# The shared expert of the last batch computed after the expert tiles of a Flamingo block, from operands kept in DRAM

## The reference, cut to what matters

```python
def _L1_ffn_ref(hidden_states, router_w, gate_w, up_w, down_w, s_gate_w, s_gate_b, s_up_w, s_up_b, s_down_w, s_down_b):
    B, S, H, I, E, TOP_K, NS = (2, 512, 512, 352, 8, 2, 2)
    ...
    logits = x @ router_w.T
    probs = jax.nn.softmax(logits.astype(jnp.float32), axis=-1)
    topk_w, topk_idx = jax.lax.top_k(probs, TOP_K)
    ...
    def expert_step(acc, ws):
        gw, uw, dw, ce = ws
        out = jax.nn.silu(x @ gw) * (x @ uw) @ dw
        return (acc + ce[:, None].astype(out.dtype) * out, None)
    moe_out, _ = jax.lax.scan(expert_step, jnp.zeros_like(x), (gate_w, up_w, down_w, combine.T))
    shared = jax.nn.silu(x @ s_gate_w + s_gate_b) * (x @ s_up_w + s_up_b) @ s_down_w + s_down_b
    return (moe_out + shared).reshape(b, s, h)
...
x = x + jnp.tanh(g_ffn[1]) * _L1_ffn_ref(_layernorm(x, axis=-1), L1_ffn_router_w, ...)
```

## Time and profile before

| | us |
|---|---|
| median of 3 runs | 1328.61 |
| lowest and highest | 1327.72, 1329.63 |
| the profiled execution's own time | 1324.98 |
| its span, first to last instruction | 1323.3 |
| PE busy | 1088.6 (82%) |
| DVE busy | 751.8 (57%) |
| ACT busy | 664.9 (50%) |
| POOL busy | 460.1 (35%) |

### The profile page before, as it was taken

How to read it: one execution, slowest core, us unless ns; L and a number is a source line. 1 busy time by engine, 2 the same in 40 slices (tenths; PEclk the granted TensorE clock), 3 DMA queues, 4 the chain that set the end, 5 groups by cost and what they waited for, 6 DMA issues and landing times. The chain is left out here.

```text
span 1323.3 us, 19258 instructions
## 1 busy us (share of the span) xinstructions
PE 1088.6 (82%) x6093; PEld 520.5 (39%) x6111; DVE 751.8 (57%) x1420; ACT 664.9 (50%) x1010; POOL 460.1 (35%) x503
## 2 busy tenths in 40 slices
PE   0567788896699999999999467899997999999910
PEld 0343444453233343243232133444444566566600
DVE  6889867756786674665653466443333435443224
ACT  6888878794156665655667154212212344334400
POOL 1102443323102332322333303435006888882054
PEclk9978899998989999999999778799998999999965
DMA  9126600001102111110110122024003454442256
GB/s 336 45 96 196 257 0 1 1 1 40 37 23 68 37 40 54 40 37 22 41 31 18 45 74 66 1 96 181 1 0 114 150 162 166 150 156 93 71 170 227
DMA packets 66573, 110.62 MB, mean 84 GB/s; under 512 B 16756, under 2 KB 28660, under 8 KB 65992
## 3 DMA queue, kind: packets, MB, share of 16 engines
q1 hardware_dynamic: 56952, 77.63, 18.2%
q0 software_dynamic: 9264, 31.92, 7.6%
q10 hardware_dynamic: 288, 0.20, 0.1%
HBM read 68.44 MB, written 33.28 MB: 77 GB/s over the span
## 5 line engine op out<-in xcount | busy, mean ns | idle before, releaser
L1240 ACT ACTIVATE prob<-p_col,mask_col,any_key 128x512 f32<-128x512 f32 x256 | 185.7, 778 | 110.4 <-PE p_col L1371 108.9
L1438 DVE CUSTOM_DVE_ANT_0 ajunk<-p_row,mask_row 128x512 bf16<-128x512 f32 x256 | 166.8, 685 | 70.8 <-PE p_row L1321 70.8
L1334 PE MATMUL p_out<-prob,v 128*64 128x512 f32 x512 | 139.0, 621 | 0.1
L1321 PE MATMUL p_row<-ks,early_place 99*128 99x512 f16 x256 | 99.3, 389 | 13.4 <-DVE top L1438 11.9
L1160 POOL TENSOR_TENSOR o<-sum_a,rec 32x512 f32<-32x512 f32 x30 | 37.9, 1264 | 195.2 <-DMA rec<-inv_d 193.0
L1371 PE MATMUL p_col<-early_place,ks 101*128 101x512 f16 x256 | 95.5, 386 | 0.7 <-ACT prob L1240 0.3
L2290 DVE SCALAR_TENSOR_TENSOR shid<-s_up,ssilu 128x352 f32<-128x352 f32 x39 | 20.5, 525 | 122.1 <-PE s_up L2236 122.1
L2258 PE MATMUL s_down<-mw,shT 128*128 (+1 forms) x351 | 82.2, 379 | 1.1 <-ACT shT L2198 1.1
L2236 PE MATMUL s_gate<-mw,sxT 128*128 x468 | 78.3, 318 | 4.2 <-ACT sxT L2204 3.3
L2236 PE MATMUL s_up<-mw,sxT 128*128 x468 | 76.7, 314 | 0.0
L1851 PE MATMUL p_gate<-mw 128*128 128x512 f16 (+1 forms) x288 | 71.7, 402 | 1.2 <-ACT mw L1737 1.2
(11 more groups left out here) (305 smaller groups left out, 2151.6 us busy)
## 6 DMA issues: line engine op xcount, KB each, us to landing
x_slots<-nought SPq DMA_DIRECT2D x3, 3328.0 KB, 19.8
xin<-x_slots SPq DMA_DIRECT2D x39, 256.0 KB, 2.7
y_slots<-y SPq DMA_DIRECT2D x39, 256.0 KB, 2.1
early_place<-in_ctx SPq DMA_DIRECT2D x8, 1024.0 KB, 5.6
mstg<-in_L_ffn_gate_w POOLq DMA_DIRECT2D x7, 704.0 KB, 5.0
mstg<-in_L_ffn_up_w POOLq DMA_DIRECT2D x7, 704.0 KB, 5.3
x<-in_x SPq DMA_DIRECT2D x4, 1024.0 KB, 6.7
w<-in_L_ffn_w SPq DMA_DIRECT2D x1, 4096.0 KB, 18.3
```

Source lines behind the costliest of these rows:

```text
L1240: nc.scalar.activation(prob[s % 4][:, c, :], p_col[c][:], ACT.Exp, bias=mask_col[:, b, k:k + 1], scale=any_key[:, b:b + 1]).then_inc(t_exp, 1)
L1321: nc.tensor.matmul(p_row[g % 2][:], qs[0:ROWS_R, j, g, t * P:(t + 1) * P], ks[b % 2][0:ROWS_R, g, :], start=True, stop=True).then_inc(t_ro ...
L1334: mm = nc.tensor.matmul(p_out[pr][c * 2 * DH:(c + 1) * 2 * DH, :], v1[b % 2][:, k, g, :], prob[n % 4][:, c, :], start=(k == 0), stop=(k == ...
L1438: nc.vector.tensor_tensor_reduce(junk[:, g % 2, :], p_row[g % 2][:], mask_row[:, blk // HPG, :], 1.0, -3e38, ALU.add, ALU.max, top[blk % 2 ...
```

## The change

The last batch (g = 3, `LATE_B`) leaves the loops of the first block on PE, ACT and DVE: its `gate_up`, `hidden`, `down` and `add` for both units are gone there. Behind its last weight load SP now writes the two split shared units and the `xT` rows of batch 3 (high and low) into two DRAM tensors, and waits for all six transfers.

In the second block the gate part of unit 0 is loaded into a tile of its own (`first_gate`) at the start. `xT` of batch 3 (`late_T`) goes into the `mstg` buffers after the last split. When PE is through with the last tile, SP loads the up part of unit 0 to the place of expert 5, stores the last `y`, and loads the rest of both units. PE, ACT and DVE then do the same products for batch 3 that stood in the first block, with hidden rows at the places of experts 4 and 7. DVE's list interleaves them with the additions of the gathered rows (`combine`). `bias` and `gate_dn` live in both blocks.

```diff
@@ stage_shared, SP: behind the weight loads
+            for u in range(2):
+                kept = w[:, (SHARED + u) * 2 * WC:(SHARED + u + 1) * 2 * WC].rearrange("p (h c) -> p h c", h=2)
+                sp.wait_ge(m_wl, NQ * (u + 1))
+                sp.dma_start(shared_d[u, :, :, 0:MAIN], kept[:, :, 0:MAIN]).then_inc(m_saved, 16)
+                sp.dma_start(shared_d[u, 0:ELAST, :, MAIN:WC], kept[0:ELAST, :, MAIN:WC]).then_inc(m_saved, 16)
+            sp.wait_ge(m_xT, NT)
+            for h in range(2):
+                sp.dma_start(late_d[h], xT[:, h, :, LATE_B * S:(LATE_B + 1) * S]).then_inc(m_saved, 16)
+            sp.wait_ge(m_saved, 16 * 6)
@@ stage_shared, PE
-            for g in range(1, B):
+            for g in range(1, LATE_B):
                 gate_up(g, 0)
                 down(g - 1, 1)
...
-            down(B - 1, 1)
+            down(LATE_B - 1, 1)
@@ stage_tiles, SP
+            sp.dma_start(first_gate[:], shared_d[0, :, :, G0:U0]).then_inc(e_pre, 16)
...
+            sp.wait_ge(m_wl, NQ * (2 + EXPERTS))
+            for h in range(2):
+                sp.dma_start(late_T[h], late_d[h]).then_inc(e_pre, 16)
             body(PAIRS_OF_TILES, 0)
+            sp.wait_ge(e_down, TILES)
+            sp.dma_start(late_w[0][:, :, U0:D0], shared_d[0, :, :, U0:D0]).then_inc(e_lu, 16)
             store(PAIRS_OF_TILES, 0)
+            sp.dma_start(late_w[1][:, :, G0:D0], shared_d[1, :, :, G0:D0]).then_inc(e_lv, 16)
+            for n, done in enumerate((e_ld0, e_ld1)):
+                sp.dma_start(late_w[n][:, :, D0:MAIN], shared_d[n, :, :, D0:MAIN]).then_inc(done, 16)
+                sp.dma_start(late_w[n][0:ELAST, :, MAIN:WC], shared_d[n, 0:ELAST, :, MAIN:WC]).then_inc(done, 16)
@@ stage_tiles, PE: behind the last tile
+            def late_gate_up(n):
...
+                        if m == 0:
+                            pe.wait_ge(*came)
+                        pe.wait_ge(free, TILES + max(c - 1, 0))
...
+            def late_down(n, done):
+                pe.wait_ge(done, 32)
+                pe.wait_ge(e_hl, TILES + EB * (n + 1))
+                for t in range(TPB):
+                    pe.wait_ge(e_y, TILES + max(TPB * n + t - 1, 0))
...
+            late_gate_up(0)
+            late_gate_up(1)
+            late_down(0, e_ld0)
+            late_down(1, e_ld1)
@@ stage_tiles, DVE: behind the last tile
+            for c in range(2 * EB):
+                late_hidden(c)
+                if c:
+                    late_low(c - 1)
+                if c == EB:
+                    combine(0)
+            late_low(2 * EB - 1)
+            combine(1)
+            late_add(0)
+            combine(2)
+            late_add(1)
+            dve.wait_ge(e_y, TILES + 2 * TPB)
+            combine(LATE_B)
```

More of the change, by code:

```diff
@@ L1791, in _ @@
             hidden(2, 1)
-            hidden(3, 0)
-            hidden(3, 1)
             act.wait_ge(m_scat, SCATTERED)
@@ L2019, in _ @@
             add(1, 0)
-            for g in range(2, B):
+            for g in range(2, LATE_B):
                 hidden(g, 0)
@@ L2031, in _, with stage_tiles @@
                     low_part(u, q)
[L2034 removed]
+def stage_tiles(nc, sb, ps, sem, st, a, x, x_slots, y_slots, out_d, w, stg, dest, share, expert_of, m_wh, m_wl,
+                bias, gate_dn, shared_d, late_d):
     NQ = len(W_PARTS)
@@ L2046, in stage_tiles @@
     identh = sb(st, "sidenth", [P, P], F16)
+    first_gate = sb(st, "first_gate", [P, 2, KB * EI], F16)
+    late_T = [stg[h][:, 0:KB * S // 2].bitcast(F16).rearrange("p (k s) -> p k s", s=S) for h in range(2)]
+    AT_HT, AT_UNIT, AT_HID = 4, 5, 7
+    late_hT = [[w[:, AT_HT * 2 * WC + (2 * n + h) * EB * S:AT_HT * 2 * WC + (2 * n + h + 1) * EB * S].rearrange("p (m s) -> p m s", s=S)
+                for h in range(2)] for n in range(2)]
+    late_silu, late_hid = ([w[:, AT_HID * 2 * WC + (2 * i + n) * 2 * S:AT_HID * 2 * WC + (2 * i + n + 1) * 2 * S].bitcast(F32)
+                            for n in range(2)] for i in range(2))
+    late_w = [w[:, (AT_UNIT + n) * 2 * WC:(AT_UNIT + n + 1) * 2 * WC].rearrange("p (h c) -> p h c", h=2) for n in range(2)]
     gathered = w[:, 0:2 * NT * D * 2].bitcast(F32).rearrange("p (t s d) -> p t s d", s=2, d=D)
```

86 lines of the change are left out of this document (69 added, 17 removed).

## The result

Four runs of each kernel: 1294.88 us after (1293.82 to 1299.26) against 1328.30 us before (1327.72 to 1329.63). The ratio is 0.9753, 95% interval 0.9729 to 0.9778: faster by 33.4 us, where 36.0 was forecast. The profiled execution of the changed kernel took 1299.26 us, span 1297.6. It is the slowest of its four, so the traces are only 25.7 us apart.

What follows compares the result with a forecast made beforehand. PE was taken to bound the first block's end, the gathers the tail. From the median 1328.61, -46.66 for batch 3's products and +10.65 in the tail, -36.0 together, gave 1292.6 us; range 1284 to 1302, chance 0.74 for the forecast.

Steps and rivals of the forecast that it cites:

- Part 1: End of the first block: taking batch 3's gate, up and down products off PE saves 46.66 us.
- Part 2: First block's writes to DRAM: hidden behind PE's rest of batch 2, cost 0, upper end 12.4 us.
- Part 3: Tile block: loading `first_gate` delays POOL's first split 2.0 us but stays hidden; cost 0, upper end 2 us.
- the 2.9 us of room: Tile block: expert 1, complete at 1033.4, is needed by PE at 1036.32 at the earliest, hiding the `first_gate` delay.
- Part 4: Tail: late products and DVE's order make PE wait, so the fourth combine starts 10.65 us later.
- best case: Low end of the forecast's own range, with no first wait and no clock drop: 1287 us.
- 2: Tail: the gathers stay the end, combine 3 starts at 1315.65, time 1284.5 us; chance 0.05.
- 5: Tail: the moved work lies behind the gathers instead of beside them; more than 10.65 of 46.66 us does.
- Rival 3: Tail: the clock stays low for all late products, each doubles, time 1326.9 us, the same; chance 0.03.
- rival P: From f2_gathers_last's forecast: a long run of 512-column products brings the slowdown by itself; time near 1365 us on such a chip.

Runs made afterwards that it cites:

- e3_writes_x3: The changed kernel with each of the six DRAM writes made three times, to other tensors, on chip 2: 1363.42 us, ratio 1.0082 to the kernel before.
- e9_fill_both: The changed kernel with unread products filling PE's gaps ahead of the first late up and third late down products, on chip 2: 1341.52 us.
- e4_add_first: The changed kernel with DVE adding the rows of each unit before combines 1 and 2, on chip 2: 1345.04 us.
- e6_up_early: The changed kernel with the first late up weights in a small tile of their own, loaded with `late_T`, on chip 2: 1336.96 us.
- f2_gathers_last: The changed kernel with POOL issuing the gathers only behind the last late up product, on chip 3: 1320.57 us.
- e1_again: The changed kernel unedited, run again on chip 2: 1343.34 us, ratio 0.9929 to the kernel before on that chip.
- f0_before: The kernel before, unedited, run again on chip 2 for a trace: 1351.3 us.
- f1_again: The changed kernel unedited, run again on chip 3: 1297.82 us, ratio 0.9769 to the kernel before.

## Why the prediction held, point by point

- **Part 1**, -46.66: the block begins 46.64 earlier once the 6.06 us of earlier stages are taken off. Right to 0.02 us, since the stretch has nothing but PE's products in it. That the 6.06 us are scatter of the earlier stages is read from the later traces on chips 2 and 3.
- **Part 2**, 0 for the writes: right. 345 to 420 GB/s, last landing near 945. Less the 6.06 us that this trace is late, that is 939 where 938 was forecast, and ten ahead of the cover's end. e3_writes_x3 shows what the cover hides.
- **Part 3**, 0 with 2 as the upper end: the tile block is 2.08 us longer (266.6 to 267.8 in nine of the ten traces with the load of `first_gate` at its start, 264.5 and 264.9 in the two of the kernel before). POOL's first split was delayed by 1.05 us, not 2.0. The step in doubt is the 2.9 us of room: it was read for one tile of expert 1, and the experts behind it were not looked at. No single later wait accounts for the 2 us, and e9_fill_both has 262.31 with the same load, so their cause stays open. `late_T` was in time, as forecast: it landed 5.5 us after its issue at 1216.58, and PE needed it at 1224.70.
- **Part 4**, +10.65: it measured 12.80. The order of events is as written; the terms of the sum were off. The up load took 5.1 us and not 4.4, so the gap was 2.62 and not 1.9 (+0.7). A gap of 2.62 did bring the low clock, by 1.7 us; I had taken none, from one row with 1.89. The first down product is thus 37.50 us after the last tile product instead of 35.15. Behind the gap of 4.48 the clock was low for longer than the 18 matmuls of the earlier trace rows had shown: 36 took 2.8 us over their full-clock 7.95, where I had 1.37. Behind the gap of 3.04 it did not fall, -1.35, but that was not a matter of the gap's length: behind the same 3.04 us the 18 products took 5.75 us in e4_add_first, e6_up_early and f2_gathers_last, about what I had taken. The fourth combine is at 64.70 instead of 62.55; so near it comes in part because these misses have opposite signs.
- **The whole.** The measured terms give -31.8 us where the sum had -36.0, and the medians are 33.4 apart. The sum of the best case was also off by one: 1292.6 - 1.9 - 2.7 is 1288, not 1287.
- The gathers start 3.0 us later relative to the last tile product (8.18 against 5.15), forecast 2.5. Beside the low parts on DVE they keep a median of 947 ns with at most 1204, so no hold of up to 4.1 us is seen, such as the prediction took from the rule of the Trainium skill's page "SBUF — State Buffer", section "Who interferes with whom".
- **The rivals.** 2 is out by the bracket of the fourth combine, 5 by PE's 49.9 us beside the gathers. Rival 3 (late products that take twice as long) named the right symptom for chip 2 with another mechanism: not a low clock for all of them, but 24 us in which they come one by one. On that chip the forecast would have failed: 8 us and not 36. Its own warning, late products of more than 2.6 us outside the stretches behind a gap, is what the trace shows there.

## What to carry to other kernels

Work that is moved beside a transfer is worth what the transfer hides, and what sticks out is set by the order of the engine that serves both; cutting that engine's long pieces brought most here (10.8 us on chip 3; filling PE's gaps brought 1.8 on chip 2, inside the spread, and the two are not to be compared directly). The first load that moved work needs belongs ahead of the work's turn: its wait was paid twice here, 2.6 us idle and 1.7 in a lower clock. Measure such a move on more than one chip: this one was worth 2.5%, 2.3% and 0.7% on three.

## What the runs showed of the hardware

- On one chip of three, matmuls came one by one, 0.7 to 3.5 us apart, while indirect DMAs (gathers into or scatters out of on-chip memory) were in flight, though PE waited for nothing in the profile. ACT and DVE took up PE's results up to 29 us late there, from about 10 us behind the first gather on (1267.53, 1282.90 and 1297.04 in e1_again). In the tail it cost 24.1 us. In the first block the way from the first scatter to the tile block was 23.5 us longer in e1_again than in the changed kernel's first trace, and 22.1 longer in f0_before than in the first trace of before. The DMA engines moved the same there as elsewhere: 205 GB/s from 910 to 920 in e1_again, 193 in the same stretch of the changed kernel on the first chip, whose products kept step.
- The end of such a stretch follows the last indirect DMA in all six tails (5.1 to 5.7 us). The first lone product comes 18.5 to 21.4 us behind the first gather, and as well 24.9 to 27.7 us behind the first late product, so the tails alone leave rival P. The first block speaks against it: in f0_before PE ran such products for 85 us behind the scatters at the full clock, and in e3_writes_x3 beside writes at 383 GB/s, with no lone one. What is left is that both are needed, products and indirect DMAs, and why only this chip shows it; f2_gathers_last on that chip would test it, and did not run there. A slow fetch of PE's instructions is not the cause by the trace: the one block fetched in the tail's stretch took 1.09 us at 1264.80, as in f1_again at 1243.11. The cause stays open. A page of the Trainium skill, "NOTIFIC — the notification-queue block", section "Overflow: three behaviours, one of which stalls the engine", says that the path for the engines' records can hold them back. No run here shows whether that is what happened, nor whether the stretch is there in an execution that nothing records.
- The granted clock was 0.50 behind gaps of 2.62 and 4.48 us but stayed at 1.00 behind one of 3.04, in the same tail and again in f1_again; behind 3.04 us in e4_add_first, e6_up_early and f2_gathers_last it did fall (5.75 us for 18 products, instead of 4.07). e9_fill_both shows that it is PE's idle time that matters, and the length of one gap alone does not say whether the level falls.
